# Memory layer of an eight-layer kernel: the weighing as tiles of 32 rows, the update as two sets of products, key sums held negative

## The reference, cut to what matters

```
qkv = xn @ w_qkv                      # xn: layer norm of x
def step(mem, z), (q_s, k_s, v_s, qn_s, kn_s):        # one segment of 32 rows
    sdpa = softmax(mask(q_s @ k_s.T * SCALE)) @ v_s   # q_s, k_s rotated (rope)
    sq, sk = elu(qn_s) + 1, elu(kn_s) + 1
    mem_out = (sq @ mem) / (sq @ z + 1e-6)
    out = beta * mem_out + (1 - beta) * sdpa
    prev_v = (sk @ mem) / (sk @ z)
    mem = mem + sk.T @ (v_s - prev_v)
    z = z + sk.sum over the 32 rows
y = out @ w_out
```

## Time and profile before

| | |
|---|---|
| median of 3 runs | 2612.66 us (2610.97 to 2617.28) |
| profiled execution, span | 2623.8 us |
| PE busy in the span | 2176.9 us (83%) |
| DVE busy | 1700.0 us (65%) |
| ACT busy | 1437.8 us (55%) |
| POOL busy | 1106.7 us (42%) |
| memory layer within the span | 1729 to 2452 us |

### The profile page before, as it was taken

How to read it: one execution, slowest core, us unless ns; L and a number is a source line. 1 busy time by engine, 2 the same in 40 slices (tenths; PEclk the granted TensorE clock), 3 DMA queues, 4 the chain that set the end, 5 groups by cost and what they waited for, 6 DMA issues and landing times. The chain is left out here.

```text
span 2623.8 us, 79243 instructions
## 1 busy us (share of the span) xinstructions
PE 2176.9 (83%) x30448; PEld 1549.2 (59%) x30448; DVE 1700.0 (65%) x5819; ACT 1437.8 (55%) x3704; POOL 1106.7 (42%) x1076
## 2 busy tenths in 40 slices
PE   6499948589964889899999977948999999999696
PEld 3288845379862233333334336937778777787396
DVE  6722247642336778787878833358999989899522
ACT  5455544355552256455455555537777767776353
POOL 2066644146654120120200004547777777776164
PEclk7699979789986799998989888969999999999798
DMA  4011120011125121111111000121111111111013
GB/s 133 33 42 43 43 85 2 33 32 44 43 93 163 55 58 31 38 39 31 35 46 35 5 33 29 41 85 54 54 53 56 52 53 55 52 56 52 35 42 92
DMA packets 76025, 134.96 MB, mean 51 GB/s; under 512 B 17225, under 2 KB 32264, under 8 KB 73224
## 3 DMA queue, kind: packets, MB, share of 16 engines
q1 hardware_dynamic: 62080, 102.07, 12.6%
q0 software_dynamic: 13568, 27.81, 3.7%
q10 hardware_dynamic: 8, 0.00, 0.0%
HBM read 65.19 MB, written 32.79 MB: 37 GB/s over the span
## 5 line engine op out<-in xcount | busy, mean ns | idle before, releaser
L1544 ACT ACTIVATE ca_pt<-ca_ps 128x512 f32<-128x512 f32 (+3 forms) x768 | 341.1, 491 | 322.3 <-PE ca_ps L1649 137.2
L734 PE MATMUL ffn_ps<-ffn_xst,ffn_up_w 128*128 128x128 f32 x3392 | 420.8, 278 | 0.2 <-issue 0.2
L734 PEld LDWEIGHTS ffn_ps<-ffn_xst,ffn_up_w 128*128 128x128 f32 x3392 | 402.9, 195 | 1.2 <-issue 1.2
L857 DVE TENSOR_TENSOR ffn_hid<-ffn_sg,ffn_ps 128x512 f32<-128x512 f32 x212 | 145.8, 688 | 359.2 <-PE ffn_ps L734 110.9
L576 POOL DMA_INDIRECT ffn_xs<-ffn_x,ffn_token_at x212 | 205.2, 968 | 301.5 <-DVE ffn_token_at L840 165.5
L581 POOL DMA_INDIRECT ffn_y<-ffn_ys,ffn_result_at x212 | 208.8, 985 | 139.2 <-DVE ffn_ys L863 82.3
L1645 PE MATMUL ca_ps<-ca_stacks 75*128 75x512 bf16 (+3 forms) x768 | 245.2, 342 | 18.3 <-ACT ca_pt L1544 10.7
L1777 DVE TENSOR_REDUCE ca_m_far<-ca_ps 128x1 f32<-128x128 f32 (+5 forms) x384 | 236.7, 616 | 30.3 <-PE ca_ps L1623 27.9
L643 ACT ACTIVATE ffn_sg<-ffn_ps 128x512 f32<-128x512 f32 x212 | 125.7, 593 | 233.6 <-remote 182.3
L1623 PE MATMUL ca_ps<-ca_stacks 72*128 72x512 bf16 (+3 forms) x768 | 223.4, 356 | 34.1 <-DVE ca_m_near L1778 21.9
L1778 DVE CUSTOM_DVE_ANT_0 ca_spill<-ca_ps,ca_bias_q 128x256 f32<-128x256 f32 (+1 forms) x512 | 201.1, 397 | 10.9 <-PE ca_ps L1623 10.9
(11 more groups left out here) (340 smaller groups left out, 4742.0 us busy)
## 6 DMA issues: line engine op xcount, KB each, us to landing
im_mates<-im_t SPq DMA_DIRECT2D x256, 128.0 KB
ffn_got<-ffn_y SPq DMA_DIRECT2D x48, 256.0 KB, 5.8
ca_stacks<-scratch_q_piece SPq DMA_DIRECT2D x16, 576.0 KB
ca_stacks<-scratch_k_piece SPq DMA_DIRECT2D x48, 192.0 KB
ffn_x<-ffn_xn SPq DMA_DIRECT2D x32, 256.0 KB, 2.0
w_w<-in_L_ffn_experts_w_dram SPq DMA_DIRECT2D x2, 2048.0 KB, 12.0
ffn_xs<-ffn_x,ffn_token_at POOLq DMA_INDIRECT x212
ffn_y<-ffn_ys,ffn_result_at POOLq DMA_INDIRECT x212
```

The costliest lines, as they stand in the source:

```text
L734: last = nc.tensor.matmul(ps[:, bank, j * P:j * P + P], up_w[:, n % WS, first + j * P:first + j * P + P], xst[:, n % 2, :], start=True, st ...
L1544: nc.scalar.activation(pt[:, i % 8, lo - c0:hi - c0], ps[:, tile_bank(i), lo - c0:hi - c0], ACT.Exp, scale=SCALE).then_inc(p_ready, 1)
```

## The change

Five edits, all in `memory_layer`. (1) `weigh` uses 32 products in place of 6: for each batch b and head parity e a tile of 32 rows by 64 columns, first m1 with a 32x32 piece of the identity, then the values with the probabilities, to bank UP + b. The probabilities need not stand apart any more: `gate_p` on POOL multiplies `pt` (128 x 128) with the head's share alone, and `own`, `own_g` and their memsets and products at the start go. (2) `uu` holds the recalled part alone, by one instruction; `learn` makes the update from two sets of 16 products each, with uu (65 elements) and with the values (64), and DVE no longer waits for the lifted values. (3) z and the recalled part change sign: the column of mem starts at -1e-6, gate[1] is negated, remember adds. (4) `weigh` now writes to banks 6 and 7 too, which hold the output parts. So it waits for the additions into x up to this step (`x_ready`), `add` moves on DVE from behind `turn_p` to behind `remember`, and `product` waits for the latest copy-out. (5) `copy_out` reads four banks in place of two.

```diff
-        b_ot = ps[:, UP:UP + PB, OT:OT + P]
-        b_out = ps[:, UP + 2:UP + 4, OT:OT + 2 * P].rearrange("p c (d f) -> p c d f", f=P)
+        b_ot = ps[:, UP:UP + BATCH, OT:OT + PB * SEG]
+        b_out = ps[:, UP + 2:UP + 4, OUT:OUT + 2 * P].rearrange("p c (d f) -> p c d f", f=P)
...
-                nc.gpsimd.memset(own[:], 0.0).then_inc(S["made"], 1)
-                for b in range(BATCH):
-                    pool.wait_ge(S["made"], 9 + b)
-                    nc.gpsimd.memset(own[SEG * b:SEG * b + SEG, b, :], 1.0).then_inc(S["made"], 1)
-                pool.wait_ge(S["made"], 13)
...
                 for q in range(NQ):
-                    for e in range(2):
-                        shape = [P, PB, BATCH, SEG]
-                        gated = nc.gpsimd.tensor_tensor(own_g[:, q, e * PB:e * PB + PB], own[:].unsqueeze(1).to_broadcast(shape),
-                                                        share[:, q * QH + e:q * QH + QH:2].unsqueeze(2).unsqueeze(3).to_broadcast(shape), ALU.mult)
+                    gated = nc.gpsimd.tensor_copy(sorted_share[:, q].rearrange("p (e k) -> p k e", e=2), share[:, q * QH:q * QH + QH].rearrange("p (k e) -> p k e", e=2))
...
-                def spread(j):
+                def gate_p(j):
                     pool.wait_ge(S["pt_ready"], j + 1)
                     if j >= 2:
                         pool.wait_ge(S["weighed"], j - 1)
-                    shape = [P, QH, BATCH, SEG]
-                    nc.gpsimd.tensor_tensor(pt_e[:, j % 2], pt[:].unsqueeze(2).to_broadcast(shape), own_g[:, j % NQ], ALU.mult).then_inc(S["pte_ready"], 1)
+                    nc.gpsimd.tensor_tensor(pt_g[:, j % 2], pt[:], bl(sorted_share[:, j % NQ], SEG), ALU.mult).then_inc(S["ptg_ready"], 1)
...
                     if j:
                         pe.wait_ge(S["ot_copied"], j)
-                    pe.wait_ge(S["pte_ready"], j + 1)
+                    if adds_by[j + 4]:
+                        pe.wait_ge(S["x_ready"], adds_by[j + 4])
+                    pe.wait_ge(S["ptg_ready"], j + 1)
                     for n in range(PB):
-                        nc.tensor.matmul(ps[:, UP + n, OT:OT + P], m1[:, j % 2, 2 * n:2 * n + 2, :].rearrange("p h d -> p (h d)"), g.ident[:], start=True, stop=False, skip_group_check=True)
-                    for n in range(PB):
-                        for e in range(2):
-                            last = nc.tensor.matmul(ps[D * e:D * e + D, UP + n, OT:OT + P], values_of(j)[:, 2 * n + e, :], pt_e[:, j % 2, PB * e + n].rearrange("p b t -> p (b t)"),
-                                                    start=False, stop=True, skip_group_check=True)
+                        heads = [(b, e, slice(SEG * b, SEG * b + SEG), ps[D * e:D * e + D, UP + b, OT + SEG * n:OT + SEG * n + SEG]) for b in range(BATCH) for e in range(2)]
+                        for b, e, tok, out in heads:
+                            nc.tensor.matmul(out, m1[tok, j % 2, 2 * n + e, :], g.ident[tok, tok], start=True, stop=False, skip_group_check=True)
+                        for b, e, tok, out in heads:
+                            last = nc.tensor.matmul(out, values_of(j)[tok, 2 * n + e, :], pt_g[tok, j % 2, PB * e + n, :], start=False, stop=True, skip_group_check=True)
...
-                    pe.wait_ge(S["ot_copied"], GROUP * i + 3 * NQ + first // PB + 1)
+                    pe.wait_ge(S["ot_copied"], min(k - 3, N))
...
-                                last = nc.tensor.matmul(b_up[half, b, blk * E1:blk * E1 + E1], keys[tok, blk, half], uu[tok, r, PB * parity + blk, :],
-                                                        start=True, stop=True, skip_group_check=True)
+                                nc.tensor.matmul(b_up[half, b, blk * E1:blk * E1 + E1], keys[tok, blk, half], uu[tok, r, PB * parity + blk, :],
+                                                 start=True, stop=False, skip_group_check=True)
+                            for b in range(BATCH):
+                                tok = slice(SEG * b, SEG * b + SEG)
+                                last = nc.tensor.matmul(b_up[half, b, blk * E1:blk * E1 + D], keys[tok, blk, half], values_of(j)[tok, 2 * blk + parity, :],
+                                                        start=False, stop=True, skip_group_check=True)
...
-                    nc.vector.tensor_tensor(m, m, b_up, ALU.subtract).then_inc(S["mem_ready"], 1)
+                    nc.vector.tensor_tensor(m, m, b_up, ALU.add).then_inc(S["mem_ready"], 1)
...
-                    dve.wait_ge(S["lifted"], j + 1)
                     if 2 <= j < LEARNED:
                         dve.wait_ge(S["upd_ready"], j - 1)
-                    for h in range(QH):
-                        e, n = h // PB, h % PB
-                        last = nc.vector.scalar_tensor_tensor(uu[:, r, h, 0:D], prev_view[:, e, n, 0:D], rd[:, h:h + 1], values_of(j)[:, 2 * n + e, :], ALU.mult, ALU.subtract)
-                    last.then_inc(S["u_ready"], 1)
+                    nc.vector.tensor_tensor(pairs(uu[:, r, :, 0:D]), prev_view[:, :, :, 0:D], over(rd[:], D), ALU.mult).then_inc(S["u_ready"], 1)
...
                     if 0 <= k - 4 < LEARNED:
                         remember(k - 4)
+                    if k in added_in:
+                        add(added_in[k])
...
                         turn_p(k - 3)
-                    if k in added_in:
-                        add(added_in[k])
```

More of the change, by code:

```diff
@@ L1857, in memory_layer @@
     PR, NU, SC = 0, PB * E1, 2 * PB * E1
-    UP, OT = 4, 192
+    UP, OT, OUT = 4, 192, 256
     N = W * NQ
@@ L1973, in _ @@
                 pool.wait_ge(S["made"], 6)
-                nc.gpsimd.memset(mem[:, :, :, :, D:E1], 1.0e-6).then_inc(S["made"], 1)
+                nc.gpsimd.memset(mem[:, :, :, :, D:E1], -1.0e-6).then_inc(S["made"], 1)
                 pool.wait_ge(S["made"], 7)
@@ L2018, in _ @@
                     if 0 <= k - 3 < N:
-                        spread(k - 3)
+                        gate_p(k - 3)
                     if k < N:
```

23 lines of the change are left out of this document (12 added, 11 removed).

## The result

The changed kernel takes 2882.73 us (median of 4 runs, 2880.46 to 2890.85); the kernel before, run beside it, 2614.97 us. The ratio is 1.103 with a 95% interval of 1.1007 to 1.1053: 268 us slower, where about no change was forecast.

A forecast was written before the change was run, and what follows sets the result against it. It took a PE-DVE ring of 5.12 us in a 5.295 us step as the bound, then late exchanged rows. Loop +3, start -5 and tail -1 gave -3 us: 2612.7 to 2609 us, range 2563 to 2636.

The forecast's parts named there:

- What is late next: Memory loop: late exchanged rows hold a two-step chain through rotation and learn; step 5.32 us against 5.295, +3 us.
- rival E: PE's small products start 25 ns apart, not 7.6: 6.5 us a step, +125 us, 2735 us; chance 0.02.
- Weighing, 1.12 to 0.68 us: Weighing on PE: 64 records of small products plus two shape turns replace six products, gain 0.44 us a step.
- uu, -0.43: DVE's uu in each step: four instructions of 0.85 us become one of 0.42 us.
- learn, +0.25 up to +0.49: Update products on PE: 16 more, 32 records, cost +0.25 us a step, at most 0.49.
- PE alone, 4.70 a step: PE's products in sequence after the change: 1.95 + 2.10 + 0.65 us; with the addition each fourth step 4.81.
- The ring: Loop chain scores, num, s1, m1, next scores through PE and DVE: 5.12 us before, 4.25 after the change.
- Late rows, L from 2.75 to 3.43: Exchanged rows' DMA lateness, sines' end to rotation, grows with x1.53 packets to 3.43 us; chain 4.93 us a step.
- Unevenness, 0.15: Added to the loop's step because the worse of two overlapping pairs of steps decides: 0.15 us.
- The start, -4.9: Memory layer's start: PE starts about 1.2 us earlier without own's memsets, el some 3.7 us sooner without own_g's products.
- The wait for the addition, nothing: Weighing's new wait holds PE some 0.2 us each fourth step; DVE is later still, so no cost.
- Rival D, half clock: PE falls to half clock inside the loop, some 1 us or more each; 2640 us or more; chance 0.06.

The follow-up runs named there:

- with 96 products more: The kernel before with six more sets of num's 16 products, one column each, every step: 3299.74 us against 2621.38, ratio 1.259.
- the run with the weighing alone: The changed kernel with the update of before, so only the weighing in 32-row tiles is new: 2704.79 us against 2564.49, ratio 1.056.
- the run with `num` first: The kernel before with num of step k-2 ahead of the weighing of step k-4, no instruction added: 2645.15 us against 2617.75, ratio 1.011.
- The run with learning alone: The kernel before with only the change's update (two sets of products, one uu instruction, negative key sums): 2615.11 us against 2564.49, ratio 1.0216.
- with fewer products: The changed kernel without the second head block's products in scores, prev and num from the fifth step: 2724.68 us against 2617.75 for before, ratio 1.040.
- the start alone: The kernel before with PE's and DVE's first waits freed of own, and own_g made behind the first four rotations: ratio 1.000 (0.998 to 1.002).
- the addition's place: The changed kernel with the addition into x put back behind turn_p, the weighing's wait kept: 2907.06 us against 2617.75 for before, ratio 1.108.

## Why the prediction was wrong, point by point

**The step that failed** is in the part "What is late next": "these are PE's own instructions, 1.2 packets a step, and they pass through the same DMA engines as the rows". The count was right. 257 records a packet was forecast and 29784 + 29785 records in 236 packets are 252; 1.9 packets a step was forecast and 236/127 = 1.86 came. What was wrong was who waits for them. I let the packets delay only `mates`, and took it as given that PE always has its next instructions. In its place the runs showed that PE itself stops at a packet's end until the next has come (154 of 158 distances between the stops are multiples of 256 records), and that over a loop they come no faster than one per 3.9 us: 929 us for the change's 236 packets, with or without the exchange of rows (919). The warning stood in my own rows: 23 packets in 100 us is 4.3 us each, and x1.53 would have asked for one each 2.8 us in a step of 5.3, without a sign that this is possible. By 3.94 the forecast's own 481 records are 481/256 x 3.94 = 7.4 us a step, +220 us by the forecast's factor of 104 steps. That factor is given no reason there; the loss falls on all 127 steps from the first sines to the last, (7.317 - 5.325) x 127 = 253 us. A rival of this form was not on the list; rival E, which had nearly as much (6.5 us a step), had it for another reason.

**The rule.** The Trainium skill, Runtime: NRT & Kernel Launch, section Instruction fetch mechanics, describes blocks of 16 KiB with 256 instructions, fetched by a queue of the sequencer's own, and says that the cost of crossing a block is "mostly hidden", since instructions are issued more slowly than they are fetched. The trace agrees with the block (16 KB, 128 matmul and 128 weight load records between two stops) and disagrees with the rest in the kernels with long rows of small products: with 96 products more PE goes through one block in 1.2 us and waits 2.5, and in the changed kernel 177 us of the loop's 929 are waits for issue.

**Weighing, 1.12 to 0.68 us.** Right but for 0.1: 0.79 where no stop falls into it, a gain of 0.33. But the turn from the value projection into it takes 0.63 us (2100.41 to 2101.04 in the run with the weighing alone) in place of 0.54, so PE's sequence gains 0.24. **The 25 ns floor (rival E).** Sixteen records of the new tile in 0.34 us, the last of them 0.2 long, start 9 ns apart: E was rightly small. **uu, -0.43.** Right: 0.41 us in place of 0.85.

```profile
2202.90 0.41 DVE L2267 TENSOR_TENSOR im_uu<-im_ps,im_rd 128x256 f32<-128x256 f32 x1
```

**learn, +0.25 up to +0.49.** Too small. The forecast had 0.40 from learn's first record to the scores, and it is 0.41 where the scores don't wait (see the run with `num` first). In the changed kernel it is 2210.61 to 2211.56, 0.95 us, so +0.54. Learn's own length, first record to end, went from 0.49 to 1.02.

```profile
2210.61 0.38 PE L2161 MATMUL im_ps<-im_uu,im_lift 32*64 32x65 f32 x13
...
2211.30 0.33 PE L2165 MATMUL im_ps<-im_lift 32*64 32x64 f32 x8
2211.56 0.60 PE L2083 MATMUL im_ps<-im_rope_qk 64*32 64x32 f32 x29
```

**PE alone, 4.70 a step.** Too low by 0.5, quite apart from the packets: PE's sequence of before without its wait for m1, with the measured sizes, is 4.90 - 0.24 + 0.54 = 5.20. The run with learning alone bears out its last term: 4.90 + 0.54 = 5.44, and its undisturbed steps take 5.44. The ring that held the old kernel was 5.12, so the change would not have gained even with its instructions at hand. This is worked out, not run; no kernel here has the change's products without their records.

**Late rows, L from 2.75 to 3.43.** POOL's wait for `mates` did rise, from 58.2 us in the loop to 169.4, but it is not what the time follows: with the weighing alone it is 176.0 and with fewer products 183.5, both more than in the changed kernel, which is slower than either, and taking the exchange out gives 0.7%. **Unevenness, 0.15.** Half of half of the 1.24 us between 4.00 and 2.76 is 0.31; it is 0.15 only when halved again, for a chain over two steps, which the text doesn't say. **The start, -4.9.** `el` begins 17.74 us after the layer's first memset in place of 22.04: -4.3 there, near the forecast; that the whole program gains it is not shown (see the start alone). **The wait for the addition, nothing.** Right: 3.0 us in the loop, see the addition's place. **Rival D, half clock.** In part: the granted clock in the loop is 0.93 against 0.99, in the run with 96 products more 0.80, and in the three windows of the last section it is low behind the two long stops at the packets. It adds to PE's busy time, but the time per packet doesn't follow it (3.94, 3.95).

What stays open is why the packets come at this pace. The runs exclude the bandwidth of the DMA engines and the rows' traffic. The traces show of what the 3.9 us consist, by the medians of the stops of over 0.4 us in the changed kernel's loop: a packet moves for 1.1 us, PE starts 1.4 us after it has landed, and the next packet starts 1.4 us after that (1.2 with 96 products more). So one packet is under way at a time, and behind such a stop the next starts only after PE has gone on. In none of the fourteen traces does a packet start sooner than 2.3 us after the one before it has landed, also where PE isn't short of instructions. Why it isn't asked for sooner, nothing here shows. Open, too, is why the kernel with `num` first is stopped at 4.56 us a packet, and how much of the 0.45 us between an undisturbed step and the mean one in the kernel with `num` first is due to stops that the trace puts down to weight loads.

## What to carry to other kernels

Count TensorE's records (a product has a load and a matmul, each twice in f32 here), and divide the time of a stretch by the packets of the instruction queue in it. If it already runs near 4 us a packet, a faster form with more and smaller products loses, whatever each of them costs, and the place to look is PE's idle time put down to issue. Before splitting a product, compute records a step / 256 x 3.9 us and compare it with the step. If it is the longer, the products' own time hardly counts; if it is the shorter, single stops can still cost, as with `num` first. And when an engine seems to have a few per cent of room, add up its sequence start to start, with the turns between the shapes as the new order will have them and without the waits that are to go, before a ring is taken for the bound.

## What the hardware showed that was not expected

- PE's instructions arrive at one packet of 256 records per 3.9 us (3.89 to 4.05 in nine kernels), 15 ns a record. In a short row PE starts the matmul records of small products 7 to 9 ns apart, each with the record of its load: 256 records in 1.2 us, 5 ns a record. No run kept that up over a loop.
- In a starved loop a packet moves for 1.1 us, PE goes on 1.4 us after it has landed, and only then does the next one start; in all fourteen traces it starts 2.3 us or more after the last has landed.
- The pace is hardly touched by other transfers: 3.94 us with 40 GB/s beside it, 3.89 with 5.
- Behind long stops the granted clock was 1.2 of 2.4 GHz. In the run with 96 products more, three windows: behind a stop of 1.03 us it is 1.00, behind one of 2.43 us (a few products lie between) and one of 2.52 us it is 0.50. Three windows make no rule. In the changed kernel the projections' records, which the change left as they were, take 309 ns on average against 278, at a mean clock of 0.93 against 0.99.

```profile
2099.60:2101.40 1.80, 1.80 (x11) 1.80 (x10) 1.62 (x9) 0.60 (x1) 0.00 (x0) 0.50 0.04 9
...
2107.70:2109.00 1.30, 1.30 (x103) 1.21 (x103) 0.20 (x1) 0.00 (x0) 0.64 (x1) 1.00 0.11 28
2119.30:2122.00 2.70, 2.70 (x75) 2.53 (x76) 1.58 (x10) 0.60 (x1) 0.00 (x0) 0.50 0.02 6
```

```profile
L2131 PE MATMUL im_ps<-im_xt_all,im_w 128*128 128x128 f32 x1016 | 160.1, 309 | 5.6 <-issue 5.6
```
